# Halo copy on another engine, a fixed choice of Z buffers, and a last block taken tile by tile with two result buffers

## The chip, the cores and the metric

One core of one Trainium2 chip runs the whole program. Times are device microseconds of one launch, from the profiler or from timed runs. Of TensorE, VectorE, ScalarE, GpSimd and SyncE (which issues most DMAs) each has its own queue of instructions; they meet only at semaphores.

## The reference, cut to what matters

Two decoder layers with post-layernorm, on x of 2 x 2048 x 512 (T = 4096 rows). Six residual blocks follow each other. The change touches the last three: the Mamba block (its projection and convolution, and its scan), and the last two blocks, attention over a context of 77 rows and an int8 matmul, which the kernel runs as one stage.

```python
# Mamba block: d_inner = 1024, d_state = 16
x_in, z = split(x @ in_proj_w.T)
x_in = silu(conv1d(x_in, width 4, 3 zeros ahead of each sequence) + conv_b)
dt, Bp, Cp = split(x_in @ x_proj_w.T);  dt = clip(softplus(dt * w + b), 1e-4, 10)
h = h * exp(dt * A) + dt * Bp * x_in          # for 16 states n, over time
y = sum_n h[n] * Cp[n]
y = (layernorm(y) * ln_g + ln_b + D * x_in) * silu(z);  out = y @ out_proj_w.T
# last two blocks
x5 = layernorm(x + softmax(q k.T / sqrt(32)) v @ Wo + bo)      # 16 heads, 77 keys
q = round(x5 / s), s = max|x5| over the row / 127
x6 = layernorm(x5 + (q @ round(rhs / rs)) * s * rs)
```

## The kernel before, in words

Everything is written out by hand: each stage opens a block with one function per engine, and the order of the calls in these functions is the order on that engine. `wait_ge(semaphore, count)` holds an engine's queue in order. P = 128, D = 512, KD = D / 128 = 4, TB = 512, NU = 4.

**Input stage** (`inner_stage`, 8 blocks of 512 time steps, 8 channel groups c of 128). In round n TensorE transposes x of block n (L1706), projects it group by group (`project`, L1714), and between groups 0 and 1 computes x_proj of block n-1 (`x_proj`, L1722) and, behind group 1, spreads its dt (L1727). ScalarE copies the transposes (`copy_xt`, L1762) and the projections into xi (`copy_xi`, L1770), applies silu for block n-1 (`silus`, L1807), logs for n-2 and Abs, Relu and Exp for n-1 (`exps`). VectorE convolves (`conv`, L1905 and L1910): xi has room for 3 columns ahead of the 512 of a block, the halo, which must hold the last 3 columns of the block before. So ahead of the convolutions of block n VectorE copies it for all 8 groups in one instruction (L2021); for block 4, the first of the second sequence, it writes zeros (L2019). xi is double-buffered. GpSimd does the middle of the softplus for n-1 (L1850 to L1863) and the product with u for n-2 (L1868).

**Scan stage** (`scan_stage`, 4 time pieces of 1024, 8 groups, 16 states n: 512 scans). GpSimd makes X = B * w (L2255), ScalarE A = exp(dt * A) (L2277), VectorE scans (L2431). The sum over n of h * C is made in three ways: for n in 0, 3, 6, 9, 12 by TensorE out of transposes (`turn`, `fold`), for 4, 7, 10 by GpSimd into Z (`outputs`, L2262), for the eight others by VectorE into Z (L2436). TensorE adds each Z to PSUM (`add`, L2379). Z has RZ = 4 buffers; `zed(k)` numbers the 11 products of a group of 16, and keeps counting from group to group, `same_z(k)` names the product that used the buffer last, and `mm` counts TensorE's adds. A second branch (`clips == 1`), not taken in this data, already chooses the buffer by `zed(n)`.

**Final stage** (`final_stage`, 8 blocks of 512 rows, each 4 tiles of 128). In round n: attention of block n, residual, layernorm and quantising of block m = n-1, int8 result of block f = n-2. TensorE: `scores`, `project` (L2888), `turn`, `queries`, `values`, `int8` (transposes L2933, matmuls L2938). VectorE: `rescale` (y6 = big * scales, L3072), `add_x5` (L3076), `residual` (L3091), statistics of r5 and y6 (L3081), `aggregate` (L3097), `inverse` (L3103), `round5` (x5 L3107, maximum L3114, scales L3116 and L3118, q5 L3122 and L3125), and the normal of y6 (L3107). ScalarE: exps, copies, one Sqrt per round (L3002), casts of q5 (L2996). SyncE stores y6 when all four tiles of it are normalised (L2838). y6 is single: `rescale(f)` waits for the store of block f-1. `project(m, a)` waits for rescale of tile a of block m-1, since both use the PSUM bank big[a]. Rounds 8 and 9 only drain the pipeline: round 8 has project, residual and `round5` of block 7 and the result of block 6, round 9 the result of block 7.

Of the kernel before, what the change touches and what calls it, by code (L numbers as in the profile page):

```python
# [1593 lines left out]
def inner_stage(nc, x3_d, ident, win_t, conv_w, conv_b, xp_t, dtw, dtb, a_log, sel_b, keepA, flag, u_d, dt_d, w_d, xd_d, xt_d):  # L1594
# [3 lines left out]
    with ExitStack() as ctx:  # L1598
# [156 lines left out]
        def _(act):  # L1755
# [133 lines left out]
        def _(dve):  # L1889
# [176 lines left out]
def scan_stage(nc, keepA, flag, ident, win_t, dt_d, w_d, xd_d, xt_d, y_d, z_d):  # L2066
# [12 lines left out]
    with ExitStack() as ctx:  # L2079
# [167 lines left out]
        def _(pool):  # L2247
# [95 lines left out]
        def _(pe):  # L2343
# [25 lines left out]
            def add(k):  # L2369
# [8 lines left out]
                for e in range(TC // TB):  # L2378
                    last = nc.tensor.matmul(yp[:, e * TB:(e + 1) * TB], idn[:], Z[:, zed(k) % RZ, e * TB:(e + 1) * TB], start=(n == FIRST), stop=(n == NS - 1))  # L2379
# [29 lines left out]
        def _(dve):  # L2409
# [5 lines left out]
            with dve.If(clips == 0):  # L2415
                for k in range(NU_):
# [15 lines left out]
                    if on_dve(n):  # L2432
                        dve.wait_ge(sn, 1 + k + 1)
                        dve.wait_ge(mm, 1 + NS + (added(same_z(k)) if zed(k) >= RZ else 0))
                        dve.wait_ge(cc[ci(n)], 1 + (i + 1) * 16)
                        nc.vector.tensor_tensor(Z[:, zed(k) % RZ], a, Cm[:, ci(n)], ALU.mult).then_inc(cd, 1)  # L2436
# [326 lines left out]
def final_stage(nc, x4_d, ident, wq, bq, wo_, bo, rhs_t, keep, out_d):  # L2763
# [5 lines left out]
    with ExitStack() as ctx:  # L2769
# [16 lines left out]
        q5, y6 = s.sb("q5", [P, NU, D]), s.sb("y6", [P, NU, D])  # L2786
# [15 lines left out]
        qtr, qte, im, ia, ib, ok, stored = [s.sem(n) for n in ("qtr", "qte", "im", "ia", "ib", "ok", "stored")]  # L2802
# [4 lines left out]
        CPB = NB // B  # L2807

# [8 lines left out]
        def _(sp):  # L2817
# [14 lines left out]
            for n in range(1, NB + 2):  # L2832
# [3 lines left out]
                if n >= 2:  # L2836
                    sp.wait_ge(ok, 1 + (n - 1) * NU)
                    sp.dma_start(orr[n - 2], y6[:]).then_inc(stored, 16)  # L2838
            sp.wait_ge(stored, 1 + NB * 16)

        @block.gpsimd
        def _(pool):
# [3 lines left out]
            for n in range(NB):  # L2846
                for a in range(NU):
# [3 lines left out]
                    nc.gpsimd.tensor_tensor(x[:, n % NX_, a], x[:, n % NX_, a], bor[:], ALU.add).then_inc(xbo, 1)  # L2851

        @block.tensor
        def _(pe):
# [85 lines left out]

            queries(0)
            pe.wait_ge(keys, 1 + HB4 * B)
            for n in range(NB + 1):
# [13 lines left out]
                if n:  # L2957
# [5 lines left out]
        def _(act):  # L2963
# [39 lines left out]

            queries(0)
            for n in range(NB + 2):
# [5 lines left out]
                if slots(n):  # L3011
# [11 lines left out]
                elif n <= NB:  # L3023
                    integers(n - 1)

        @block.vector
        def _(dve):
# [39 lines left out]
            def rescale(f):  # L3067
                dve.wait_ge(stored, 1 + f * 16)
                dve.wait_ge(wte, 3)
                for a in range(NU):  # L3070
                    dve.wait_ge(im, 1 + f * NU + a + 1)
                    nc.vector.scalar_tensor_tensor(out=y6[:, a], in0=big[:, a], scalar=ls[:, a:a + 1], in1=rg[:], op0=ALU.mult, op1=ALU.mult).then_inc(ia, 1)  # L3072

            def add_x5(f, a):
                dve.wait_ge(ia, 1 + f * NU + a + 1)
                nc.vector.tensor_tensor(y6[:, a], y6[:, a], x5[:, a], ALU.add).then_inc(ib, 1)  # L3076
# [7 lines left out]
            def stats_y6(f, a):  # L3084
                dve.wait_ge(ib, 1 + f * NU + a + 1)
                stats_of(1, a, y6)
# [40 lines left out]
            for n in range(NB + 2):  # L3127
# [30 lines left out]
                if old:  # L3158
                    for a in range(NU):
                        normal(y6[:, a], y6[:, a], 1, a).then_inc(ok, 1)  # L3160
                if n == 0:
                    weights()

# [80 lines left out]
```

## Time and profile before

| what | value |
|---|---|
| median of 3 runs | 4980.63 us (4979.41 to 4981.1) |
| the profiled execution's own time | 4978.69 us |
| its span, first to last instruction | 4976.9 us |
| busy share TensorE, VectorE, ScalarE, GpSimd | 85%, 71%, 45%, 53% |
| mean granted TensorE clock | 0.935 |

The page divides the span by engine and in 40 slices; a share is an average over stages with different limits. The input stage lies at about 2160 to 2580 us, the scan at 2585 to 4100, the final stage at 4420 to 4977. A timeline row gives start, duration, engine, line, operation, result and operands, how many instructions are merged in it, and in brackets how long the engine idled before and what released it.

### The profile page before, as it was taken

What the parts mean: (1) busy time and instruction counts of PE and PEld (TensorE: products, weight loads), DVE (VectorE), ACT (ScalarE), POOL (GpSimd) and SP (SyncE); (2) the same over time, 40 slices, a digit from 0 to 9 for tenths busy, and PEclk for the clock granted to TensorE, in tenths of its full rate; (3) what the DMA queues carried; (4) which work ended last, traced back from release to release, by engine and by line L of the source; (5) the groups of instructions that cost most, each with busy time, mean ns of one, the idle gap of its engine ahead of it and who ended that gap; (6) DMA issues with size and microseconds to landing.
All of it is one profiled execution on the core that took longest, in us unless ns stands there. A gap on an engine that the chain in (4) does not pass through costs nothing. (4 is left out here: it accounts for less than half of the span.)

```text
span 4976.9 us, 49426 instructions
## 1 busy us (share of the span) xinstructions
PE 4217.4 (85%) x16117; PEld 2401.9 (48%) x16117; DVE 3526.9 (71%) x3880; ACT 2218.5 (45%) x3950; POOL 2654.5 (53%) x1555
## 2 busy tenths in 40 slices
PE   8997987599999459979837988888888888978886
PEld 6776875344444124433314555555555543435553
DVE  5554337522277555559978999999999997955676
ACT  1211114322255631037755676666766664423442
POOL 4544965100033011118868999999999986622221
PEclk9998996599999779989969999999999999989998
DMA  3332233242278765425453242242242217630100
GB/s 106 105 95 63 79 100 118 76 155 87 101 280 299 290 265 203 152 96 196 162 191 118 70 133 100 70 142 91 71 157 75 70 41 268 228 115 18 34 26 34
DMA packets 364162, 632.15 MB, mean 127 GB/s; under 512 B 67478, under 2 KB 153271, under 8 KB 351746
## 3 DMA queue, kind: packets, MB, share of 16 engines
q1 hardware_dynamic: 326850, 585.97, 33.7%
q10 hardware_dynamic: 37056, 43.00, 2.4%
q8 instruction: 132, 2.16, 0.2%
q14 instruction: 124, 1.02, 0.1%
HBM read 400.73 MB, written 228.15 MB: 126 GB/s over the span
## 5 line engine op out<-in xcount | busy, mean ns | idle before, releaser
L2255 POOL TENSOR_TENSOR sc_X<-sc_Bm,sc_w 128x1024 f32<-128x1024 f32 x512 | 1192.3, 2364 | 101.4 <-DVE sc_A L2431 42.1
L2379 PE MATMUL sc_yp<-sc_Z,sc_idn 128*128 128x512 f32 x1408 | 674.5, 602 | 23.2 <-DVE sc_Z L2436 21.4
L1329 PE MATMUL ff_ps<-ffn_R 128*128 128x512 f32 x1536 | 660.6, 592 | 0.7 <-issue 0.7
L2277 ACT ACTIVATE sc_A<-sc_dt,keep_A 128x1024 f32<-128x1024 f32 x512 | 575.2, 1123 | 162.4 <-DVE sc_Z L2436 84.2
L1329 PEld LDWEIGHTS ff_ps<-ffn_R 128*128 128x128 f32 x1536 | 291.2, 190 | 364.5 <-issue 363.8
L2307 ACT ACTIVATE sc_hT<-sc_tp,sc_ct 128x128 f32<-128x128 f32 x1280 | 362.8, 366 | 173.2 <-PE sc_tp L2359 172.2
L2379 PEld LDWEIGHTS sc_yp<-sc_Z,sc_idn 128*128 128x128 f32 x1408 | 248.5, 191 | 272.9 <-issue 209.1
L2366 PEld LDWEIGHTS sc_yp<-sc_idn,sc_hT 128*128 128x128 f32 x2560 | 306.6, 192 | 113.3 <-ACT sc_hT L2307 80.9
L2366 PE MATMUL sc_yp<-sc_idn,sc_hT 128*128 128x128 f32 x2560 | 318.1, 278 | 15.7 <-ACT sc_hT L2307 15.7
L2436 DVE TENSOR_TENSOR sc_Z<-sc_A,sc_Cm 128x1024 f32<-128x1024 f32 x256 | 313.5, 1225 | 8.9
L2431 DVE TENSOR_TENSOR_SCAN sc_A<-sc_A,sc_X 128x1024 f32<-128x1024 f32 x128 | 292.1, 2282 | 31.7 <-ACT sc_A L2277 28.9
L73 POOL TENSOR_TENSOR gp_pbd<-gp_r,gp_msk 128x512 f32<-128x512 f32 x144 | 182.2, 1265 | 236.4 <-DVE gp_r L474 236.4
L2431 DVE TENSOR_TENSOR_SCAN sc_A<-sc_A,sc_hc,sc_X 128x1024 f32<-128x1024 f32 x128 | 299.6, 2341 | 2.3 <-ACT sc_A L2277 2.3
L2359 PE MATMUL sc_tp<-sc_idn,sc_H 128*128 128x128 f32 x1280 | 196.0, 276 | 119.4 <-DVE sc_A L2431 71.7
L2431 DVE TENSOR_TENSOR_SCAN sc_H<-sc_A,sc_hc,sc_X 128x1024 f32<-128x1024 f32 x128 | 295.2, 2337 | 1.1 <-ACT sc_A L2277 1.1
L2431 DVE TENSOR_TENSOR_SCAN sc_H<-sc_A,sc_X 128x1024 f32<-128x1024 f32 x128 | 287.2, 2274 | 11.6 <-POOL sc_X L2255 11.6
L2388 PE MATMUL sc_zp<-sc_xz,sc_wz 128*128 128x512 f32 x512 | 266.0, 601 | 28.9 <-issue 17.8
L1357 PE MATMUL ff_ps<-ffn_downT,ffn_R 128*128 128x512 f32 x672 | 289.3, 593 | 0.4 <-DVE ffn_R L1538 0.4
L2359 PEld LDWEIGHTS sc_tp<-sc_idn,sc_H 128*128 128x128 f32 x1280 | 150.1, 141 | 286.6 <-issue 175.9
L1373 ACT ACTIVATE ff_o<-ff_ps,ff_scx 128x512 f32<-128x512 f32 x192 | 129.0, 683 | 333.5 <-PE ff_ps L1329 320.7
L2849 POOL TENSOR_TENSOR fi_pr<-fi_pr,fi_rp 128x1232 f32<-128x1232 f32 x32 | 71.9, 2248 | 375.2 <-DVE fi_rp L3065 375.2
L1453 DVE TENSOR_REDUCE ff_amg<-ff_o 128x1 f32<-128x512 f32 x96 | 65.5, 686 | 269.8 <-ACT ff_o L1373 269.7
(379 smaller groups left out, 8083.0 us busy)
## 6 DMA issues: line engine op xcount, KB each, us to landing
sc_Bm<-d_xd SPq DMA_DIRECT2D x64, 512.0 KB, 7.5
ffn_gate_d<-ff_o SPq DMA_DIRECT2D x96, 256.0 KB, 2.2
ffn_up_d<-ff_o SPq DMA_DIRECT2D x96, 256.0 KB, 6.3
ffn_g_d<-ff_z SPq DMA_DIRECT2D x24, 1024.0 KB, 6.7
ffn_R<-ffn_g_d SPq DMA_DIRECT2D x8, 3072.0 KB, 11.0
ffn_R<-ffn_up_d SPq DMA_DIRECT2D x8, 3072.0 KB, 21.6
ffn_R<-ffn_up_d SPq DMA_DIRECT2D x23, 1024.0 KB, 12.8
sc_Cm<-d_xd SPq DMA_DIRECT2D x44, 512.0 KB, 8.2
```

Of the source, the lines that this page charges most:

```text
L73: return eng.tensor_tensor(out.rearrange("p g (c m) -> p g c m", m=16), packed.unsqueeze(2).broadcast_to([P, n, CH, 16]), mask.rearrange(" ...
L1329: last = nc.tensor.matmul(ps[:, 2 + t % 6], w[:, k, h * P:(h + 1) * P], xt[:, n, k], start=(k == 0), stop=(k == KD - 1))
L1357: last = nc.tensor.matmul(ps[:, v * NU + u], zd[v][:, k, u * P:(u + 1) * P], downT[:, k], start=(k == 0), stop=(k == HB_ - 1))
L2255: nc.gpsimd.tensor_tensor(X[:, k % RX], Bm[:, n], w[:, j % 2], ALU.mult).then_inc(db, 1)
L2277: nc.scalar.activation(A[:, k % 2], dt[:, j % 2], ACT.Exp, scale=keepA[:, n:n + 1]).then_inc(ex, 1)
L2307: nc.scalar.activation(hT[:, q], tp[:, b * P:(b + 1) * P], ACT.Copy, scale=ct[:, i % 2, q, n:n + 1]).then_inc(tc, 1)
L2359: last = nc.tensor.transpose(tp[:, b * P:(b + 1) * P], H[:, slot(k % NS), h * TB + b * P:h * TB + (b + 1) * P], idn[:])
L2366: last = nc.tensor.matmul(yp[:, b * P:(b + 1) * P], hT[:, b], idn[:], start=False, stop=False)
L2379: last = nc.tensor.matmul(yp[:, e * TB:(e + 1) * TB], idn[:], Z[:, zed(k) % RZ, e * TB:(e + 1) * TB], start=(n == FIRST), stop=(n == NS - 1))
L2388: nc.tensor.matmul(zp[:], wz[:, q], xz[:, q], start=(q == 0), stop=(q == KD - 1)).then_inc(zm, 1)
L2431: nc.vector.tensor_tensor_scan(h, a, X[:, k % RX], 0.0 if first else hc[:, k % CU:k % CU + 1], ALU.mult, ALU.add).then_inc(sn, 1)
L2436: nc.vector.tensor_tensor(Z[:, zed(k) % RZ], a, Cm[:, ci(n)], ALU.mult).then_inc(cd, 1)
```

## The change

**Input stage.** ScalarE gets `copy_halo(n + 1)`, issued behind `copy_xi(n, 7)`, for all blocks but 0 and 4. VectorE keeps only the memset of block 4.

**Scan stage.** The Z buffer is `zed(n) % RZ`, so every group of 16 begins at buffer 0, in both branches, and `same_z(k)` is rewritten to match: buffers 0, 1, 2 have three users in a group, buffer 3 has two.

**Final stage.** y6 becomes two buffers, and `stored` two semaphores. The rounds 8 and 9 are replaced by an order written out per tile (`last_blocks` on VectorE, `last_int8` on TensorE, the list of roots and casts on ScalarE); each tile has its own aggregation, root, reciprocal, scales and quantising. The four adds of x5 for block 6 move to GpSimd. Block 7 is stored tile by tile.

```diff
+            def copy_halo(n):                              # input stage, ScalarE
+                act.wait_ge(rev, 1 + n * RG)
+                act.wait_ge(cv, 1 + (n - 1) * CB)
+                nc.scalar.copy(xi[:, n % 2, :, 0:3], xi[:, (n - 1) % 2, :, TB:TB + 3]).then_inc(halo, 1)
...
                         copy_xi(n, c)
+                    if c == CB - 1 and n + 1 < NB and n + 1 != NB // B:
+                        copy_halo(n + 1)
...
-                if n:
+                if n == NB // B:
                     dve.wait_ge(cv, 1 + (n - 1) * CB)
-                if n == NB // B:
                     nc.vector.memset(xi[:, n % 2, :, 0:3], 0.0).then_inc(halo, 1)
-                elif n:
-                    nc.vector.tensor_copy(xi[:, n % 2, :, 0:3], xi[:, (n - 1) % 2, :, TB:TB + 3]).then_inc(halo, 1)
...
         def same_z(k):
-            zs = [m for m in range(NS) if not on_pe(m)]
-            p = zs.index(k % NS) - RZ
-            return (k // NS + p // NZ) * NS + zs[p % NZ]
+            users = [m for m in range(NS) if not on_pe(m) and zed(m) % RZ == zed(k % NS) % RZ]
+            p = users.index(k % NS) - 1
+            return (k // NS + p // len(users)) * NS + users[p]
...
-                        nc.vector.tensor_tensor(Z[:, zed(k) % RZ], a, Cm[:, ci(n)], ALU.mult).then_inc(cd, 1)
+                        nc.vector.tensor_tensor(Z[:, zed(n) % RZ], a, Cm[:, ci(n)], ALU.mult).then_inc(cd, 1)
...
-        q5, y6 = s.sb("q5", [P, NU, D]), s.sb("y6", [P, NU, D])
+        q5, y6 = s.sb("q5", [P, NU, D]), s.sb("y6", [P, 2, NU, D])
...
+            for a in range(NU):                            # SyncE
+                sp.wait_ge(ok, 1 + F * NU + a + 1)
+                sp.dma_start(orr[F, :, a], y6[:, F % 2, a]).then_inc(stored[F % 2], 16)
...
+            for a in range(NU):                            # GpSimd, F = NB - 1
+                pool.wait_ge(ia, 1 + (F - 1) * NU + a + 1)
+                nc.gpsimd.tensor_tensor(y6[:, (F - 1) % 2, a], y6[:, (F - 1) % 2, a], x5[:, a], ALU.add).then_inc(ib, 1)
...
+                pe.wait_ge(res, 1 + NB * NU - 1)           # TensorE, last_int8
+                turn_q(0)
+                turn_q(1)
+                multiply(0)
+                multiply(1)
+                turn_q(2)
+                multiply(2)
+                pe.wait_ge(res, 1 + NB * NU)
+                turn_q(3)
+                multiply(3)
...
+            root_r5(0)                                     # ScalarE
+            root_r5(1)
+            root_y6(F - 1)
+            root_r5(2)
+            last_integer(0)
+            last_integer(1)
+            last_integer(2)
+            root_r5(3)
+            last_integer(3)
+            for a in range(NU):
+                root_y6(F, a)
...
+            def spread_r5(a):                              # VectorE; spread_y6 is its like
+                dve.wait_ge(res, 1 + F * NU + a + 1)
+                stats_of(0, a, r5)
+                dve.wait_ge(stats, 1 + counted[0])
+                nc.vector.bn_aggr(mv[:, 0, a], st[:, 0, a]).then_inc(eag, 1)
...
+            def last_blocks():
+                f = F - 1
+                rescale(f)
+                residual(F, 0)
+                spread_r5(0)
+                spread_y6(f, 0)
+                spread_y6(f, 1)
+                round_tile(0)
+                residual(F, 1)
+                spread_r5(1)
+                spread_y6(f, 2)
+                spread_y6(f, 3)
+                round_tile(1)
+                residual(F, 2)
+                spread_r5(2)
...
+                for a in range(NU):
+                    normal(y6[:, f % 2, a], y6[:, f % 2, a], 1, a).then_inc(ok, 1)
+                round_tile(2)
+                residual(F, 3)
+                spread_r5(3)
+                rescale_tile(F, 0)
+                add_x5(F, 0)
+                round_tile(3)
+                spread_y6(F, 0)
+                for a in range(1, NU):
+                    rescale_tile(F, a)
+                    add_x5(F, a)
+                    finish_tile(F, a - 1)
+                    spread_y6(F, a)
+                finish_tile(F, NU - 1)
```

`round_tile(a)` holds, for one tile, the reciprocal of the root, x5, its maximum, the two scales and the two quantising steps; `finish_tile(f, a)` the reciprocal and the normal of y6; each of their instructions waits for the one before.

## Rows read from the trace of the kernel before

**Rows 1.** Busy time by stretch, input stage: stretch, its length, busy us per engine.
```profile
core 0: us, PE busy (x) PEld busy (x) DVE busy (x) ACT busy (x) POOL busy (x), PEclk, DMA share, GB/s
2235.00:2282.00 47.00, 43.09 (x98) 17.39 (x98) 46.11 (x51) 34.07 (x56) 38.89 (x41) 0.90 0.50 180
...
2330.00:2373.00 43.00, 39.81 (x99) 15.98 (x97) 40.41 (x56) 33.94 (x57) 38.76 (x40) 0.96 0.55 197
```

**Rows 2.** The halo copy, by its line and as a group (count, busy, mean ns, idle).
```profile
L2021 DVE COPY in_xi<-in_xi x6: 173/7956/9009, 2192.5 to 2474.1; 128x24 f32<-128x24 f32 x6
...
L2021 DVE COPY in_xi<-in_xi 128x24 f32<-128x24 f32 x6 | 41.2, 6868 | 0.0
```

**Rows 3.** Timeline of VectorE in the input stage.
```profile
2287.51 7.24 DVE L2021 COPY in_xi<-in_xi 128x24 f32<-128x24 f32 x1
...
2334.80 0.08 DVE L2019 MEMSET in_xi<- 128x24 f32 x1
...
2376.51 8.87 DVE L2021 COPY in_xi<-in_xi 128x24 f32<-128x24 f32 x1
...
2520.66 0.75 DVE L1910 SCALAR_TENSOR_TENSOR in_acc<-in_xi,in_cw,in_ac 128x512 f32<-128x512 f32 x1
```

**Rows 4.** Timeline of GpSimd near the copy that begins at 2287.51.
```profile
2293.44 1.27 POOL L1858 TENSOR_TENSOR in_E<-in_E,in_Wm 128x512 f32<-128x512 f32 x1
2294.79 1.27 POOL L1863 TENSOR_TENSOR in_V<-in_V,in_E 128x512 f32<-128x512 f32 x1
```

**Rows 5.** Timeline of TensorE: first project matmuls of blocks 2, 4, 5, 7; transposes.
```profile
2235.04 6.67 PE L1714 MATMUL in_ps<-in_xt,in_win 128*128 128x512 f32 x8 [0.68 <-ACT in_xt L1762]
...
2329.58 5.40 PE L1714 MATMUL in_ps<-in_xt,in_win 128*128 128x512 f32 x8 [0.68 <-ACT in_xt L1762]
...
2371.11 1.14 PE L1706 MATMUL in_ps<-in_idn,in_x 128*128 128x128 f32 x8 [1.69 <-ACT in_xt L1762]
2372.93 3.70 PE L1714 MATMUL in_ps<-in_xt,in_win 128*128 128x512 f32 x8 [0.68 <-ACT in_xt L1762]
...
2468.87 3.70 PE L1714 MATMUL in_ps<-in_xt,in_win 128*128 128x512 f32 x8 [0.67 <-ACT in_xt L1762]
```

**Rows 6.** ScalarE's copies of one column, as a group.
```profile
L2289 ACT COPY sc_hc<-sc_H 128x1 f32<-128x1 f32 x49 | 9.6, 197 | 22.7 <-DVE sc_H L2431 20.2 <-ACT sc_yo L2313 2.4
```

**Rows 7.** Scan stage: the products into Z, and their timeline between two groups.
```profile
L2436 DVE TENSOR_TENSOR sc_Z<-sc_A,sc_Cm 128x1024 f32<-128x1024 f32 x256 | 313.5, 1225 | 8.9
...
3118.58 1.23 DVE L2436 TENSOR_TENSOR sc_Z<-sc_A,sc_Cm 128x1024 f32<-128x1024 f32 x1
...
3119.88 1.88 PE L2379 MATMUL sc_yp<-sc_Z,sc_idn 128*128 128x512 f32 x4
...
3131.40 1.23 DVE L2436 TENSOR_TENSOR sc_Z<-sc_A,sc_Cm 128x1024 f32<-128x1024 f32 x1
```

**Rows 8.** Timeline of the last rounds of the final stage.
```profile
4920.79 3.62 PE L2938 MATMUL fi_big<-fi_rq,fi_qbt 128*128 128x512 bf16 x16
...
4926.09 2.73 DVE L3072 SCALAR_TENSOR_TENSOR fi_y<-fi_big,fi_ls,fi_rg 128x512 f32<-128x512 f32 x4 [4.38 <-DMA out<-fi_y]
...
4926.98 15.67 PE L2888 MATMUL fi_big<-fi_wo,fi_att 128*128 128x512 f32 x32 [2.58 <-DVE fi_y L3072]
...
4932.39 0.69 DVE L3091 TENSOR_TENSOR fi_r<-fi_big,fi_x 128x512 f32<-128x512 f32 x1 [2.38 <-PE fi_big L2888]
...
4969.26 0.18 DVE L3103 RECIPROCAL fi_rstd<-fi_sd 128x4 f32<-128x4 f32 x1 [0.36 <-ACT fi_sd L3002]
4969.47 1.92 DVE L3107 TENSOR_SCALAR fi_y<-fi_y,fi_mv,fi_rstd 128x512 f32<-128x512 f32 x4
```

**Rows 9.** Groups of VectorE's instructions in the final stage.
```profile
L3081 DVE BATCH_NORM_STATS2 fi_st<-fi_y 128x6 f32<-128x512 f32 x32 | 20.3, 680 | 0.0
...
L3107 DVE TENSOR_SCALAR fi_y<-fi_y,fi_mv,fi_rstd 128x512 f32<-128x512 f32 x32 | 15.3, 545 | 0.0
```

**Rows 10.** DMA issues: count, KB each, median us to landing.
```profile
d_dt<-in_Wm SPq DMA_DIRECT2D x25, 256.0 KB, 2.3
...
out<-fi_y SPq DMA_DIRECT2D x2, 1024.0 KB, 4.3
```

More of the change, by code:

```diff
@@ L2378, in add @@
                 for e in range(TC // TB):
-                    last = nc.tensor.matmul(yp[:, e * TB:(e + 1) * TB], idn[:], Z[:, zed(k) % RZ, e * TB:(e + 1) * TB], start=(n == FIRST), stop=(n == NS - 1))
+                    last = nc.tensor.matmul(yp[:, e * TB:(e + 1) * TB], idn[:], Z[:, zed(n) % RZ, e * TB:(e + 1) * TB], start=(n == FIRST), stop=(n == NS - 1))
                 last.then_inc(mm, 1)
@@ L2801, in final_stage @@
             "om", "res", "stats", "aggr", "root", "rsd", "x5ok", "la", "lb", "lc", "qa", "qk")]
-        qtr, qte, im, ia, ib, ok, stored = [s.sem(n) for n in ("qtr", "qte", "im", "ia", "ib", "ok", "stored")]
+        qtr, qte, im, ia, ib, ok = [s.sem(n) for n in ("qtr", "qte", "im", "ia", "ib", "ok")]
+        stored = [s.sem(f"stored{v}") for v in range(2)]
+        eag, ert, ers, ex5, ela, elb, elc, eqa, eqk, eyg, eyt, eys = [s.sem(n) for n in (
+            "eag", "ert", "ers", "ex5", "ela", "elb", "elc", "eqa", "eqk", "eyg", "eyt", "eys")]
         s.start()
@@ L2807, in final_stage @@
         CPB = NB // B
+        F = NB - 1
         def slots(n):
@@ L2939, in int8, with last_int8, turn_q, multiply @@
                     last.then_inc(im, 1)
+            def last_int8():
+                def turn_q(a):
+                    pe.wait_ge(eqk, 1 + a + 1)
+                    for k in range(KD):
+                        last = nc.tensor.transpose(big[:, a, k * P:(k + 1) * P], q5[:, a, k * P:(k + 1) * P], idn[:])
+                    last.then_inc(qtr, 1)
+                def multiply(a):
+                    pe.wait_ge(qte, 1 + F * NU + a + 1)
+                    for k in range(KD):
+                        last = nc.tensor.matmul(big[:, a], qbt[:, a, k], rq[:, k], start=(k == 0), stop=(k == KD - 1))
+                    last.then_inc(im, 1)
+                pe.wait_ge(res, 1 + NB * NU - 1)
[8 more added lines that the diff above has]
+                multiply(3)
             queries(0)
@@ L2956, in _ @@
                     values(n)
-                if n:
+                if n == NB:
+                    last_int8()
+                elif n:
                     int8(n - 1)
@@ L3002, in roots, with root_r5, root_y6, last_integer @@
                 nc.scalar.activation(sd[:, used], mv[:, used, :, 1], ACT.Sqrt, bias=eps[:]).then_inc(root, 1)
+            def root_r5(a):
+                act.wait_ge(eag, 1 + a + 1)
+                nc.scalar.activation(sd[:, 0, a:a + 1], mv[:, 0, a, 1:2], ACT.Sqrt, bias=eps[:]).then_inc(ert, 1)
+            def root_y6(f, a=None):
+                us = slice(0, NU) if a is None else slice(a, a + 1)
+                act.wait_ge(eyg, 1 + NU + (0 if a is None else a + 1))
+                nc.scalar.activation(sd[:, 1, us], mv[:, 1, us, 1], ACT.Sqrt, bias=eps[:]).then_inc(eyt, 1)
+            def last_integer(a):
+                act.wait_ge(im, 1 + F * NU)
+                act.wait_ge(qtr, 1 + F * NU + a + 1)
+                nc.scalar.copy(qbt[:, a].rearrange("p k t -> p (k t)"), big[:, a]).then_inc(qte, 1)
             queries(0)
-            for n in range(NB + 2):
+            for n in range(NB + 1):
                 if n < NB:
@@ L3010, in _ @@
                     turned(n, 1)
-                if slots(n):
+                if slots(n) and n < NB:
                     roots(n)
@@ L3125, in round5, with spread_y6 @@
                     nc.vector.tensor_scalar(q5[:, a], q5[:, a], MAGIC, None, ALU.subtract).then_inc(qk, 1)
-            for n in range(NB + 2):
+            def spread_r5(a):
[3 more added lines that the diff above has]
+                nc.vector.bn_aggr(mv[:, 0, a], st[:, 0, a]).then_inc(eag, 1)
+            def spread_y6(f, a):
+                stats_y6(f, a)
+                dve.wait_ge(stats, 1 + counted[0])
+                nc.vector.bn_aggr(mv[:, 1, a], st[:, 1, a]).then_inc(eyg, 1)
@@ new lines, in round_tile @@
+            def round_tile(a):
+                dve.wait_ge(ert, 1 + a + 1)
+                nc.vector.reciprocal(rstd[:, 0, a:a + 1], sd[:, 0, a:a + 1]).then_inc(ers, 1)
+                dve.wait_ge(ers, 1 + a + 1)
+                dve.wait_ge(ib, 1 + (F - 1) * NU + a + 1)
+                normal(x5[:, a], r5[:, a], 0, a).then_inc(ex5, 1)
+                dve.wait_ge(ex5, 1 + a + 1)
+                nc.vector.tensor_reduce(lm[:, a:a + 1], x5[:, a], AX.X, ALU.max, apply_absolute_value=True).then_inc(ela, 1)
+                dve.wait_ge(ela, 1 + a + 1)
+                nc.vector.tensor_scalar(ls[:, a:a + 1], lm[:, a:a + 1], 1e-12, 1.0 / 127.0, ALU.max, ALU.mult).then_inc(elb, 1)
+                dve.wait_ge(elb, 1 + a + 1)
+                nc.vector.reciprocal(li[:, a:a + 1], ls[:, a:a + 1]).then_inc(elc, 1)
+                dve.wait_ge(elc, 1 + a + 1)
+                dve.wait_ge(qtr, 1 + F * NU)
+                nc.vector.tensor_scalar(q5[:, a], x5[:, a], li[:, a:a + 1], MAGIC, ALU.mult, ALU.add).then_inc(eqa, 1)
+                dve.wait_ge(eqa, 1 + a + 1)
+                nc.vector.tensor_scalar(q5[:, a], q5[:, a], MAGIC, None, ALU.subtract).then_inc(eqk, 1)
@@ new lines, in finish_tile @@
+            def finish_tile(f, a):
+                dve.wait_ge(eyt, 1 + 1 + a + 1)
+                nc.vector.reciprocal(rstd[:, 1, a:a + 1], sd[:, 1, a:a + 1]).then_inc(eys, 1)
+                dve.wait_ge(eys, 1 + 1 + a + 1)
+                normal(y6[:, f % 2, a], y6[:, f % 2, a], 1, a).then_inc(ok, 1)
[14 more added lines that the diff above has]
+                spread_r5(2)
+                dve.wait_ge(eyt, 2)
+                nc.vector.reciprocal(rstd[:, 1], sd[:, 1]).then_inc(eys, 1)
+                dve.wait_ge(eys, 2)
+                for a in range(NU):
+                    normal(y6[:, f % 2, a], y6[:, f % 2, a], 1, a).then_inc(ok, 1)
+                round_tile(2)
[11 more added lines that the diff above has]
+                finish_tile(F, NU - 1)
@@ L3128, in _ @@
+            for n in range(NB):
                 m, f = n - 1, n - 2
```

30 lines of the change are left out of this document (17 added, 13 removed).

## The prediction

> **What bounds the kernel now.** The diff touches three stages, so I read first the busy time of each engine in stretches of those stages, and then, inside a stretch, the timeline of the engine with the least idle time. In the Mamba input stage (about 2160 to 2580 us) VectorE is busy for 46.1 of 47 us in a block that begins with a halo copy, and for 40.4 of 43 us in block 4, which has a memset in its place [rows 1]. VectorE is the bound there. The copy moves 24 numbers per partition; it takes 173 ns once and up to 9009 ns otherwise, 41.2 us for all six [rows 2]. What the reader is to see in the two timelines: the copy begun at 2287.51 lasts 7.24 us, to 2294.75, and GpSimd, back to back until then, has a gap just from 2294.71 to 2294.79 [rows 3, 4]. The copy waits for GpSimd to pause; the 173 ns one is the first, at 2192.5, when GpSimd had no work yet.
>
> In the scan stage the 256 products of VectorE into Z have 8.9 us of idle time before them, 0.035 us each, and no releaser is named: that is the price of depending on the instruction before, not a wait for a buffer [rows 7]. In the final stage the y6 buffer costs something only at the end: rescale of block 6 idles 4.38 us for a store [rows 8], that of block 7 about as long again, and then four tiles go through each step together, so that TensorE, ScalarE and VectorE take turns.
>
> **Part 1, halo copy to ScalarE.** Six copies leave VectorE; five of them were stalled, 41.2 - 0.2 = 41.0 us together [rows 2]. All of it is saved only while VectorE stays the bound, so what is late next? TensorE's rounds (first project matmul of a block to that of the next) tell: from block 4 to 5, where nothing stalls VectorE, 2372.93 - 2329.58 = 43.35 us; the five rounds from block 2 to 7 take 2468.87 - 2235.04 = 233.8 us, so the other four 47.6 on average [rows 5]. Within a round TensorE and ScalarE hand over to each other: transposes wait 1.69 us for ScalarE's xt copies [rows 5], and x_proj for all eight silus. VectorE, when in time, has no part in it, so 43.35 us is the next bound.
>
> The new copy stands between ScalarE's last xi copy and its last exps, ahead of those xt copies, so its whole length is added to a round. What it waits for is there already: ScalarE's own xi copies, and the convolutions of the block before, for which its silus have waited earlier in the round. Queued behind it are one exps group and the xt copies. ScalarE's copy of a single column takes 197 ns [rows 6]; for 24 columns and the wait for its own last write I take 0.3 us (nearest to that row; bounds 0.2 and, three times the row, 0.6). The round of block 4 began with eight matmuls in 5.40 us, that of block 5 with 3.70 [rows 5], a clock matter that x_proj's wait for the silus mostly absorbs; so I use 43.5 us. Five rounds are 217.5 us, gain 16.3. In block 7 the last convolution ended at 2520.66 + 0.75 = 2521.4, 52.5 us after its round began; in block 4 that span is 2376.51 - 2329.58 = 46.9 us [rows 3, 5]; gain 5.6. Together 21.9; with block 2 begun 0.3 us later and something lost behind, 21. All that follows (silu, x_proj, softplus, stores) hangs on that last convolution, so the gain reaches the end of the stage. Bounds: rounds of 45.05 us (43.35 + 1.7, the clock's part not absorbed) give 8.5 + 5.6 = 14; with VectorE still the bound and block 4's idle time of 41.7 - 40.4 = 1.3 us back in each of five blocks, 41.0 - 6.5 = 34.
>
> Here a rule speaks against me. The traced copy outlasts single GpSimd instructions, of 1.27 us each [rows 3, 4]. The Trainium skill (SBUF — State Buffer, section SBUF: two separate sides) says that VectorE and GpSimd share a port pair under an exclusive lock, kept for one whole instruction, while ScalarE never waits for another engine. The second half would make the plan work. By the first half the port explains one GpSimd instruction per copy at most, 5 x 1.27 = 6 us of the 41, and the rest would be the copy's own and could move along with it; an estimate by it is a gain of 6 us here in place of 21. I follow the trace.
>
> **Part 2, Z buffers chosen by n.** Eleven products per 16 states rotate over four buffers. Now every group starts again at buffer 0, so its first three writes (n = 1, 2, 4) wait for an add three writes back, not four. For n = 1 that is the add of n = 13. Product 13 runs from 3118.58, its add from 3119.88 to 3121.76, and the next group's first product begins at 3131.40 [rows 7]: 9.6 us to spare. n = 2 waits for 14, both about 4 us later, and n = 4 is GpSimd's and later still. Cost 0, hidden by the scans of VectorE in between; each microsecond of TensorE's lag beyond 9.6 would count 31 times. A gain is excluded, as nothing waited.
>
> **Part 3, final stage.** (a) Two y6 buffers: rescale of block 6 starts when TensorE's first product is there, about 4921.7, not at 4926.09, and block 7's project follows the int8 products at once, at 4920.79 + 3.62 = 4924.4 in place of 4926.98 [rows 8]. Its first tile took 5.41 us (to 4932.39) with slow matmuls after 2.58 us of idling; without that idling eight take 3.7 [rows 5, 8]. So the first residual starts at 4928.1 (4929.8 if the clock drops all the same). The four adds of x5 for block 6 go to GpSimd, done by about 4928 while VectorE waits for TensorE: hidden, at some 1.3 us each.
> (b) From there VectorE is the bound, with TensorE and ScalarE beside it tile by tile. Its work, each instruction behind the one before, 0.035 us added: 4 residuals, 12 statistics, 4 maxima, 4 adds and 4 rescales, all near the statistics' 0.68 us [rows 9], 28 x 0.71 = 19.9; 12 aggregations, 9 reciprocals and 8 scale operations near the 0.18 us reciprocal [rows 8], together 5.5; 8 single normals at 0.57 [rows 9] and 4 in 1.92 us [rows 8], 6.5; 8 quantising steps at that 0.48, 3.8; one wait for ScalarE's root, 0.4 [rows 8]. Sum 36.1, end 4964.2. The last product is in time: tile 3's integers leave VectorE near 4953, transposes, cast and matmuls of one tile take under 4 us, and its rescale comes near 4960.
> (c) Now the last normals end at 4969.47 + 1.92 = 4971.4 [rows 8] and the span 5.5 us later, behind a store of 1024 KB that lands in 4.3 us; one of 256 KB lands in 2.3 [rows 10]. New end 4964.2 + 5.5 - 2.0 = 4967.7, gain 9.2. Bounds: 4 (clock down, 1.7, and 0.05 us more for each of some 70 waits, 3.5) and 11 (the small operations as short as in groups now).
>
> **Sum.** The profiled execution took 4978.69 us around a span of 4976.9. 4978.7 - 21 - 9.2 = 4948.5. It stands 1.9 us under the median of 4980.63, so I expect a median of 4950.5.
>
> **The rivals.** 1: VectorE stays the bound, rounds near 41.7 us. For it: its own pace in block 4 [rows 3]. Against: TensorE's 43.35 at the same place. Gain 34 + 9: 4937.5.
> 2: the rounds stretch, by TensorE's clock, a ScalarE copy of 0.6 us (4 x 0.3 more) or GpSimd's chain (38.8 of 43 us busy in block 4 [rows 1]). Rounds near 45.3, gain 13 here and 7 at the end: 4960.5. Against: block 4 shows all three engines at the fast pace once.
> 3: the copy is slow by itself. 7 to 9 us then stand inside TensorE's round in four of the five, 51 us each: 4 x 51 + 43.4 = 247 against 233.8, 5.6 back, 9 at the end: 4979, no change. For it: it outlasts single GpSimd instructions. Against: the 173 ns [rows 2].
> 4, the other side: Z's shorter distance. Place: the first product of each group. Price: 31 times what TensorE lags beyond 9.6 us. From 1.0 us per group it eats the gain, from 1.3 the kernel is slower by 10 us; with 1.5 us it is 4950 + 47 = 4997. For it: TensorE is close to full in the scan. Against: the add begins 0.07 us after its product ends [rows 7].
>
> **Chances.** Forecast 0.64, rival 1 0.13, rival 2 0.17, rival 3 0.03, rival 4 0.03. The range is 4938 to 4963, from about rival 1 to just past rival 2 and to the poor bounds of both gains (14 + 4). A change under 0.2% (10 us) can't be told from none here. Faster 0.94, the same 0.04 (rival 3 and a sliver of 2), slower 0.02.
>
> **What would show it.** No copy on VectorE in the input stage, six on ScalarE of 0.2 to 0.3 us; TensorE's rounds at 43 to 44 us, VectorE idling some 2 us per block for xi; the last convolution 21 us earlier; Z products as before; project of block 7 right behind the int8 products at the full clock; the last normal 7 us earlier counted from the stage's start. I am wrong if ScalarE's copies take microseconds, if rounds stay at 47 us, or if TensorE gates Z.

## The result, and the profile after

The changed kernel takes 4949.78 us (median of 4 runs, 4948.61 to 4953.84) against 4980.86 us (4 runs, 4979.41 to 4982.02) of the kernel before: a ratio of 0.9941, 95% interval 0.9929 to 0.9953. That is 31 us less. The profiled execution took 4948.61 us around a span of 4946.8, which is 30.1 less than before. Medians, where given, are of all runs and ratios of the undisturbed ones; three runs in the whole study were disturbed, at 5914.69 and 13430.14 us with the tensor_scalar copy below and at 5926.08 us of the kernel before beside it.

I set the same events of both traces beside each other. Each line is a stretch between two events, in us, of one profiled execution of each kernel.

| stretch, from event to event | before | after | change |
|---|---|---|---|
| start of the trace to the first convolution's last step | 2167.81 | 2165.55 | -2.3 |
| to the start of the last convolution's last step | 352.85 | 333.15 | -19.7 |
| to the first scan | 75.62 | 75.40 | -0.2 |
| to the last scan | 1496.40 | 1495.70 | -0.7 |
| to the first matmul of the final stage | 336.74 | 337.55 | +0.8 |
| to the final stage's last table load on ScalarE | 478.37 | 481.75 | +3.4 |
| to the end of the last normal | 63.60 | 54.34 | -9.3 |
| to the end of the span | 5.51 | 3.36 | -2.2 |

The input stage. Busy time of two rounds of TensorE, as in [rows 1]; the columns are stretch, length, busy time of TensorE, its weight loads, VectorE, ScalarE and GpSimd, TensorE's granted clock, the DMA share and GB/s:

```profile
2233.12:2277.26 44.14, 41.29 (x99) 16.72 (x99) 38.97 (x53) 34.60 (x58) 39.11 (x40) 0.93 0.53 192
...
2321.00:2364.00 43.00, 39.96 (x98) 16.30 (x98) 39.25 (x54) 34.20 (x58) 39.21 (x41) 0.96 0.54 197
```

VectorE is down from 46.1 us to 39.0 in a block with a halo copy. The copy itself, now on ScalarE, by its line and as a group, the answer to [rows 2]:

```profile
L1776 ACT COPY in_xi<-in_xi x6: 218/218/221, 2187.1 to 2447.4; 128x24 f32<-128x24 f32 x6
...
L1776 ACT COPY in_xi<-in_xi 128x24 f32<-128x24 f32 x6 | 1.3, 219 | 0.2
```

TensorE's transposes and first project matmuls of its rounds, the answer to [rows 5]:

```profile
2233.12 6.58 PE L1714 MATMUL in_ps<-in_xt,in_win 128*128 128x512 f32 x8 [0.68 <-ACT in_xt L1762]
2275.43 1.15 PE L1706 MATMUL in_ps<-in_idn,in_x 128*128 128x128 f32 x8 [1.93 <-ACT in_xt L1762]
2277.26 6.70 PE L1714 MATMUL in_ps<-in_xt,in_win 128*128 128x512 f32 x8 [0.68 <-ACT in_xt L1762]
2319.45 1.15 PE L1706 MATMUL in_ps<-in_idn,in_x 128*128 128x128 f32 x8 [1.69 <-ACT in_xt L1762]
2321.26 5.19 PE L1714 MATMUL in_ps<-in_xt,in_win 128*128 128x512 f32 x8 [0.68 <-ACT in_xt L1762]
2364.47 3.70 PE L1714 MATMUL in_ps<-in_xt,in_win 128*128 128x512 f32 x8 [0.68 <-ACT in_xt L1762]
2405.85 1.67 PE L1706 MATMUL in_ps<-in_idn,in_x 128*128 128x128 f32 x8 [1.93 <-ACT in_xt L1762]
2408.19 6.09 PE L1714 MATMUL in_ps<-in_xt,in_win 128*128 128x512 f32 x8 [0.68 <-ACT in_xt L1762]
2452.25 6.25 PE L1714 MATMUL in_ps<-in_xt,in_win 128*128 128x512 f32 x8 [0.68 <-ACT in_xt L1762]
```

The five rounds are 44.14, 44.00, 43.21, 43.72 and 44.06 us, 43.83 on average. The halo copy shows directly: where there is one, the transposes wait 1.93 us for ScalarE's xt copies, where there is none (ahead of block 4) 1.69. What lies over 43.2 goes with slow matmuls about the start of a round: three rounds begin with eight matmuls in 6.1 to 6.7 us in place of 3.7 (granted clock of the first round shown 0.93, of the one of 43.21 us 0.96), and the round of 43.72 us, which begins with 3.70, ends with eight transposes in 1.67 us in place of 1.15.

VectorE now waits for ScalarE's xi at the head of every block, where it had 0.9 us of idle time in a whole block [rows 1]; the rows are its first convolution step of blocks 3 and 4:

```profile
2284.62 0.81 DVE L1913 TENSOR_SCALAR in_ac<-in_xi,in_cw,in_cb 128x512 f32<-128x512 f32 x1 [3.95 <-ACT in_xi L1770]
...
2327.30 0.81 DVE L1913 TENSOR_SCALAR in_ac<-in_xi,in_cw,in_cb 128x512 f32<-128x512 f32 x1 [2.36 <-ACT in_xi L1770]
```

The scan stage. The 256 products into Z, against [rows 7]:

```profile
L2441 DVE TENSOR_TENSOR sc_Z<-sc_A,sc_Cm 128x1024 f32<-128x1024 f32 x256 | 313.5, 1225 | 8.8
```

The end of the final stage, against [rows 8]: the timeline from rescale of block 6 to the last normal, and the four stores.

```profile
4903.61 2.96 DVE L3143 SCALAR_TENSOR_TENSOR fi_y<-fi_big,fi_ls,fi_rg 128x512 f32<-128x512 f32 x4 [0.61 <-PE fi_big L2955]
4904.44 4.94 POOL L2868 TENSOR_TENSOR fi_y<-fi_y,fi_x 128x512 f32<-128x512 f32 x4 [10.30 <-DVE fi_y L3143]
4905.54 13.90 PE L2905 MATMUL fi_big<-fi_wo,fi_att 128*128 128x512 f32 x32
4909.18 0.69 DVE L3162 TENSOR_TENSOR fi_r<-fi_big,fi_x 128x512 f32<-128x512 f32 x1 [2.61 <-PE fi_big L2905]
4909.90 0.69 DVE L3152 BATCH_NORM_STATS2 fi_st<-fi_r 128x6 f32<-128x512 f32 x1
4910.63 0.18 DVE L3202 BATCH_NORM_AGGREGATE fi_mv<-fi_st 128x2 f32<-128x6 f32 x1
4910.73 0.66 DVE L3152 BATCH_NORM_STATS2 fi_st<-fi_y 128x6 f32<-128x512 f32 x1
...
4942.69 0.16 DVE L3229 RECIPROCAL fi_rstd<-fi_sd 128x1 f32<-128x1 f32 x1 [0.36 <-ACT fi_sd L3054]
4942.89 0.55 DVE L3178 TENSOR_SCALAR fi_y<-fi_y,fi_mv,fi_rstd 128x512 f32<-128x512 f32 x1
```

```profile
out<-fi_y SPq DMA_DIRECT2D x4, 256.0 KB, 2.0
```

Rescale no longer waits for a store, project follows the int8 products at the full clock (13.90 us for 32 matmuls at a granted clock of 1.00, before 15.67 at 0.89), and from 4909.18 on VectorE has a single idle time that a releaser ends, the 0.36 us ahead of the last reciprocal.

One stretch got longer although the change hardly touches it: from the first matmul of the final stage to the last table load. Its first 22 us differ in the granted clock, 0.95 before and 0.80 after (the third number from the end; the first row is of the kernel before, the second of the changed one):

```profile
4430.00:4452.00 22.00, 19.12 (x55) 10.00 (x53) 1.34 (x1) 6.38 (x9) 0.00 (x0) 0.95 0.60 222
```

```profile
4408.00:4430.00 22.00, 20.50 (x51) 10.39 (x50) 0.00 (x0) 6.22 (x9) 0.00 (x0) 0.80 0.59 219
```

Over all profiles of this study that stretch takes 478.1 to 478.9 us ten times and 481.4 to 481.9 four times. The first 22 us after the stage's first matmul have a granted clock of 0.79 in those four and of 0.92 to 0.94 in the ten. All four are of kernels with the new final stage, but five more kernels with it are among the ten. And nearly all of the difference is there by the stage's first residual, which starts 90.4 to 90.6 us after the first matmul in the four and 86.9 to 87.9 in the ten. Up to there no instruction that reads or writes y6 has run. So I don't count the 3.4 us as a price of the new code; why the clock falls early in some executions and not in others stays open.

### The profile page after: what moved, and what is told of

It reads as the page before. It is cut to its first block and busy times, and to the rows that moved or that the text cites. A ratio compares the mean times of both kernels' runs of the same rounds, so it can differ in the third digit from the quotient of the medians.

```text
span 4946.8 us, 49497 instructions
## 1 busy us (share of the span) xinstructions
PE 4213.3 (85%) x16109; PEld 2399.2 (48%) x16117; DVE 3486.8 (70%) x3883; ACT 2222.8 (45%) x3963; POOL 2659.8 (54%) x1559
## 3 DMA queue, kind: packets, MB, share of 16 engines
q8 instruction: 132, 2.16, 0.2%
```

## Experiments: the parts by themselves

Times are medians beside runs of the kernel before on the same chip. Totals of one kernel scatter by some 5 us to either side, so I also give the input stage (the second line of the table, 352.85 us before) and the tail (the seventh, 63.60 us).

**Halo copy alone**: `inner_stage` of the changed kernel, all else as before.

> The kernel before with the halo copy on ScalarE alone. My theory: this is two thirds of the gain. Its input stage is that of the changed kernel (TensorE's rounds near 43.8 us, last convolution about 20 us earlier counted from the stage's start), time 4961. Rival (the final stage or the Z buffers bring the main part, the input stage's gain is lost in the scan): under 8 us, time 4973 or more.

4963.31 us, ratio 0.9967 (0.9954 to 0.9979), 16.8 us less; input stage 334.07 us, tail 63.54. The part gives its 18.8 us of the input stage where it was expected.

**Final stage alone**: `final_stage` of the changed kernel.

> The kernel before with the new final stage alone. My theory: the tail from the last root table load of the steady rounds to the end is 57.7 us in place of 69.1, so 11.4 us less, time 4969.5. Rival (part of that is luck of the clock at the start of the last blocks): 7 to 9 us less, 4972 to 4974.

4970.03 us, ratio 0.9982 (0.9972 to 0.9992); input stage 351.67, tail 54.36 us, and 3.4 us from the last normal to the end of the span in place of 5.5. As expected.

**Z buffers alone**: `scan_stage` of the changed kernel.

> The kernel before with the Z buffers chosen by n alone. My theory: nothing waits, the scans from first to last take 1496.4 us as before, time 4980.9 within 2. Rival (the shorter distance costs, but is hidden in the sum by another gain): each microsecond of wait per group is 31 us, so 4985 or more, with idle time ahead of the products into Z above 8.9 us.

4980.06 us, ratio 1.0001 (0.9991 to 1.001). Its 256 products have 8.9 us of idle time, as in [rows 7]. No cost, no gain. The tail of this profile is 65.32 us with the old final stage, where three others with that stage have 63.5 to 63.6: from 4902 to 4928 us TensorE's granted clock was 0.67, in the kernel before 0.99. So the old tail moves by 1.7 us with the clock; all nine new ones lie within 54.28 to 54.37 us.

**Two y6 buffers alone**, in the old order of the rounds:

```diff
-        q5, y6 = s.sb("q5", [P, NU, D]), s.sb("y6", [P, NU, D])
+        q5, y6 = s.sb("q5", [P, NU, D]), s.sb("y6", [P, 2, NU, D])
...
-                dve.wait_ge(stored, 1 + f * 16)
+                dve.wait_ge(stored[f % 2], 1 + f // 2 * 16)
```

> The kernel before with two y6 buffers and nothing else: order, whole-block store and engines as they were. My theory: block 7's project starts 2.6 us earlier and at the full clock (1.9 us more), and the last rescale starts when its first product is there: old 4960.96 against products from 4957.3, so 2 to 3 us; together 5 to 7 us of the 11.4, time 4974 to 4976. Rival (the per-tile order brings nearly all, the buffers only uncover other waits): 0 to 2 us, 4979 to 4981.

4972.2 us, ratio 0.9991 (0.9982 to 1.0001). The median is 8.0 us lower, more than the 5 to 7 expected, but the interval of the ratio just takes in 1, so the runs alone don't tell this from no change. The trace tells more. The tail is 58.04 us, 5.6 less than before, within the 5 to 7 expected, and VectorE idles 0.25 us ahead of rescale, for TensorE's product, not 4.38 us for a store:

```profile
4920.76 3.24 DVE L3074 SCALAR_TENSOR_TENSOR fi_y<-fi_big,fi_ls,fi_rg 128x512 f32<-128x512 f32 x4 [0.25 <-PE fi_big L2940]
```

So of the 9.3 us of the tail the second buffer gives 5.6 and the rest of the new final stage, the order tile by tile with the four adds on GpSimd, 3.7; these last two were not run apart. Behind the tail the small stores give 2.1: with one store for the block this run still takes 5.6 us from the last normal to the end.

## Experiments: why the copy was slow, and what bounds the rounds now

The reduction, the lighter GpSimd, the added VectorE work and the copy between the xt copies were timed on another chip, where the kernel before took 4978.4 us; across chips the ratios compare, not the times.

**Another instruction for the copy, on VectorE.** A reduction over an axis of one element moves the same 24 numbers, at the old place in VectorE's queue:

```diff
-                    nc.vector.tensor_copy(xi[:, n % 2, :, 0:3], xi[:, (n - 1) % 2, :, TB:TB + 3]).then_inc(halo, 1)
+                    nc.vector.tensor_reduce(xi[:, n % 2, :, 0:3], xi[:, (n - 1) % 2, :, TB:TB + 3].unsqueeze(3), AX.X, ALU.max).then_inc(halo, 1)
```

(the rest is the changed kernel without `copy_halo` on ScalarE)

> The changed kernel with the halo back on VectorE, but as a tensor_reduce over an axis of one element, which computes the same. Theory A (the old copy waited because GpSimd and a two-port copy exclude each other; VectorE now has 2 to 4 us to spare per block): the six reductions take about 0.2 us each, rounds are 0.24 us shorter than in the changed kernel (ScalarE freed), time 4949 to 4950, about 1 us less. Rival (any VectorE operation from SBUF to SBUF at that place, or this access pattern, stalls): 5 to 9 us each, rounds of 47 us, time 4970.

4946.37 us, ratio 0.9935 (0.9921 to 0.9948), input stage 330.90 us.

```profile
L2020 DVE TENSOR_REDUCE in_xi<-in_xi x6: 173/174/176, 2194.2 to 2457.1; 128x24 f32<-128x24 f32 x6
```

All six take 173 to 176 ns beside the same GpSimd work. So neither the data, nor the access pattern, nor the place, nor a wait for the convolutions is enough to make such an instruction slow, and moving it to ScalarE was not needed for the gain. The interval overlaps the changed kernel's; its rounds are shorter in the trace (below).

**The copy kept, GpSimd lightened.** The kernel before, with `less_one`, `lost` and `relu_plus` on 8 of 512 columns, so most of the softplus is left out.

> The kernel before, where GpSimd's less_one, lost and relu_plus in the input stage work on 8 of 512 columns (the softplus is left incomplete), so that GpSimd has gaps while the halo copy is due; the copy stays a VectorE copy. Theory (the copy waits for GpSimd's first gap): copies of 0.2 to 1.3 us, rounds of 43 to 44 us, and more saved at the end of the stage where GpSimd shares the work: time 4960 or less. Rival (the copy is slow by itself in a full pipeline, for its access pattern or for DMA traffic): still 7 to 9 us each, rounds of 47 us, gain at the stage's end only, 4970 to 4978.

4948.47 us, ratio 0.9937 (0.9922 to 0.9952); input stage 330.91 us (the stretch behind it shortens too, from 75.6 to 67.7 us, with the lighter softplus, so 8 us of the total aren't the copy's).

```profile
L2021 DVE COPY in_xi<-in_xi x6: 173/174/175, 2194.9 to 2457.7; 128x24 f32<-128x24 f32 x6
```

The very instruction that took up to 9009 ns takes 174. The stall comes from GpSimd's work. This run answers a second question: its five rounds take 217.0 us together, as with the reduction beside the full GpSimd work (217.0). So GpSimd is not what bounds the rounds now.

**Is it the copy, or a class?** The same place, once as `tensor_scalar(..., 1.0, None, ALU.mult)`, once as `tensor_tensor(x, x, ALU.max)`.

> The changed kernel with the halo copy on VectorE once more, written as tensor_scalar (times 1.0) of the same 24 numbers, one input from SBUF. Known by now: as a copy it takes 7 to 9 us while GpSimd works, as a tensor_reduce 0.17 us at the same place. Theory: the stall belongs to the plain elementwise forms of VectorE with one fp32 input (copy and tensor_scalar alike), not to the name of the instruction; then five of the six take 7 to 9 us again, the rounds of TensorE average 46 to 47 us, and the time is about 4968 to 4971 (only the final stage's gain is left). Rival: it is the copy alone; then 0.17 us each, rounds of 43.0 to 43.9 us, 4946 to 4950.

> The same place, the halo copy as tensor_tensor (maximum of the 24 numbers with themselves), two inputs from SBUF. Theory: such an instruction waits for one GpSimd instruction at most, as the 1.0 to 1.2 us that small tensor_tensors of 128x8 take near 2555 us suggest where their like takes 0.16; then 0.2 to 1.3 us each, VectorE's idle time of 2.4 to 4 us per block covers it, and the time is 4946 to 4951. Rival: it waits for a gap of GpSimd like the copy; 7 to 9 us each, about 4968 to 4971.

4970.36 us (ratio 0.998, 0.997 to 0.999) and 4969.56 us (0.998, 0.9971 to 0.9989); input stages 351.50 and 352.89 us.

```profile
L2020 DVE TENSOR_SCALAR in_xi<-in_xi x6: 174/7270/9021, 2190.7 to 2470.9; 128x24 f32<-128x24 f32 x6
```

```profile
L2020 DVE TENSOR_TENSOR in_xi<-in_xi x6: 177/8000/9004, 2195.5 to 2477.0; 128x24 f32<-128x24 f32 x6
```

The first came as expected; for the second my theory fell: two inputs wait as long as one. What all have in common is where they end. Here VectorE's instruction and GpSimd's around it:

```profile
2236.65 9.02 DVE L2020 TENSOR_SCALAR in_xi<-in_xi 128x24 f32<-128x24 f32 x1
```

```profile
2243.15 1.26 POOL L1863 TENSOR_TENSOR in_V<-in_V,in_E 128x512 f32<-128x512 f32 x1
2244.37 1.27 POOL L1858 TENSOR_TENSOR in_E<-in_E,in_Wm 128x512 f32<-128x512 f32 x1
2245.71 1.27 POOL L1863 TENSOR_TENSOR in_V<-in_V,in_E 128x512 f32<-128x512 f32 x1
```

GpSimd's instructions start before the one ahead of them has ended (2243.15 + 1.26 is past 2244.37), until the last two of a block, where L1863 depends on L1858 and there are 0.07 us between them (2245.64 to 2245.71). VectorE's instruction ends at 2245.67, inside that gap. It is so for all 30 stalled ones, five each of the kernel before, of these two, and of the kernels with the final stage, the Z buffers and the two y6 buffers alone: they end at this one pair of lines, whenever they began. Most lie across 8 or 10 GpSimd instructions and last 7.2 to 9.1 us; one, begun later, lies across 6 and lasts 6.0. VectorE's 512-column instructions in the same stage are not held at all. In the kernel before the middle convolution steps take 0.756 us in the median both where GpSimd is busy throughout (80 of them) and where it is idle (23), and the tensor_scalar of L1933 takes 0.685 against 0.682. Why these pass and the 24-number ones wait stays open; none of these runs varied the shape.

**More work on VectorE.** The changed kernel, with three reductions of 128 x 512 on a scratch tile behind `extremes(m)`.

> The changed kernel with three more reductions of 0.68 us (2.0 us) on VectorE in each of seven blocks of the input stage, on a scratch tile, with no one waiting for them. Theory (TensorE and ScalarE set the rounds, VectorE idles 2.4 to 4 us ahead of each block): rounds unchanged, VectorE's idle time before a block 2 us shorter; only block 7 and what follows it see their 2 us; time 2 us above the changed kernel. Rival (VectorE is the bound still): 7 x 2.0 = 14 us more.

4949.79 us, ratio 0.9938 (0.9923 to 0.9953); the five rounds take 219.9 us together, 219.1 in the changed kernel. The input stage takes 335.95 us, 2.8 more, of which about 2 were expected in block 7, with no next round to hide in; 14 in all would have come had VectorE been the bound. VectorE's idle time took up the rest:

```profile
2374.75 0.82 DVE L1917 TENSOR_SCALAR in_ac<-in_xi,in_cw,in_cb 128x512 f32<-128x512 f32 x1 [2.13 <-ACT in_xi L1772]
```

Still 2.1 us idle here and 1.2 to 2.1 at the other heads, with about 2.0 us of work added per block (0.67 us each): VectorE is not the bound.

**Less work on ScalarE**, on top of the reduction: Abs and Exp of channel group 7 on 8 of 512 columns from the third block on, which leaves out part of the softplus.

> Halo as a reduction on VectorE, and ScalarE's Abs and Exp of channel group 7 on 8 of 512 columns from the third block on: this leaves out part of the softplus of that group. These two stand between the last xi copy of a round and the silus, and shrink by about 0.5 us each. Theory: the hand-over between ScalarE and TensorE bounds the rounds, so those at the full clock shorten from 42.95 to about 41.9 us for the blocks concerned, four or five of them: some 4 to 5 us less in the input stage, time about 4942 to 4944. Rival: VectorE (its work is 41.7 us in a block without halo copy) or GpSimd bounds as well; then the rounds stay within 0.3 us of 42.95 and the time at 4946 to 4948.

4941.93 us, ratio 0.9927 (0.9912 to 0.9943); input stage 325.49 us. Three starts of rounds (block 4 to 6), and two of the kernel with the full Abs and Exp (blocks 5 and 6):

```profile
2322.24 3.70 PE L1714 MATMUL in_ps<-in_xt,in_win 128*128 128x512 f32 x8 [0.68 <-ACT in_xt L1762]
2364.35 3.70 PE L1714 MATMUL in_ps<-in_xt,in_win 128*128 128x512 f32 x8 [0.67 <-ACT in_xt L1762]
2406.47 3.70 PE L1714 MATMUL in_ps<-in_xt,in_win 128*128 128x512 f32 x8 [0.68 <-ACT in_xt L1762]
```

```profile
2367.59 5.15 PE L1714 MATMUL in_ps<-in_xt,in_win 128*128 128x512 f32 x8 [0.68 <-ACT in_xt L1762]
2410.54 3.70 PE L1714 MATMUL in_ps<-in_xt,in_win 128*128 128x512 f32 x8 [0.68 <-ACT in_xt L1762]
```

42.11 us against 42.95, so 0.84 less. From start to start the shortened Abs and Exp take 0.26 and 0.10 us in place of 0.67 and 0.52, together 0.83 less: what is taken from ScalarE between the last xi copy and the silus comes off the round. ScalarE with its hand-over to TensorE is the bound.

**The copy between the xt copies**: `copy_halo(n)` on ScalarE behind the second xt copy, where ScalarE would wait for TensorE's transposes anyway.

> The changed kernel with ScalarE's halo copy moved from behind the last xi copy to between the second and third xt copy of the next block, where ScalarE idled 0.26 us. Theory (rounds are set by the hand-over of TensorE and ScalarE, and the copy is on it where it stands now): TensorE's wait for xt falls from 1.93 to 1.69 us, rounds shorten by up to 0.24 us, 1 us in all, time 4949; the copy's 0.2 us may show ahead of the last xt copies, then nothing. Rival (VectorE is the bound): no change, and VectorE's waits for xi as they are.

4951.37 us, ratio 0.9945 (0.9931 to 0.9958); input stage 329.93 us, the shortest with all the work in it. Its rounds are 43.91, 42.96, 43.21, 43.72 and 42.96: 42.96 without the lower clock, against 43.21 in the changed kernel. The 0.25 us of the copy are gone from the round; 4951.37 us is not below the 4949 expected, and a total that scatters by 5 us can't show so little.

**Tail: more for GpSimd.** On top of the reduction, the four normals of block 6 and one addition of block 7 move from VectorE to GpSimd:

```diff
+            pool.wait_ge(eys, 2)
+            for a in range(NU):
+                nc.gpsimd.tensor_scalar(y6[:, (F - 1) % 2, a], y6[:, (F - 1) % 2, a], mv[:, 1, a, 0:1], rstd[:, 1, a:a + 1], ALU.subtract, ALU.mult).then_inc(okg, 1)
+            pool.wait_ge(ia, 1 + F * NU + 1)
+            nc.gpsimd.tensor_tensor(y6[:, F % 2, 0], y6[:, F % 2, 0], x5[:, 0], ALU.add).then_inc(ib, 1)
```

> Halo as a reduction on VectorE (4946.4 measured), and in the tail of the final stage five more operations on GpSimd, which is idle there: the four normals of y6 of block 6 (1.92 us of VectorE) and the addition of x5 to tile 0 of block 7 (0.6 us). Theory: VectorE is the bound of the tail, so the stretch from ScalarE's last table load to the last normal shrinks from 54.4 by 2.4 to 2.5 us, to 51.9, and the time to about 4944. Rival: while GpSimd works for some 2.5 us on the normals, VectorE's single normals and quantising steps stall behind it, up to those 2.5 us; then 54 to 54.5 us and no change against 4946.4.

4947.95 us, ratio 0.9937 (0.9924 to 0.9951); tail 54.28 us in place of 54.37. Nothing gained, where 2.4 to 2.5 us were expected. The rival's time came, but only in part by its cause:

```profile
L2869 POOL TENSOR_SCALAR fi_y<-fi_y,fi_mv,fi_rstd 128x512 f32<-128x512 f32 x4 | 8.6, 2156 | 13.7 <-DVE fi_rstd L3252 13.7
```

```profile
4924.21 0.95 DVE L3226 TENSOR_SCALAR fi_q<-fi_x,fi_li 128x512 f32<-128x512 f32 x1
...
4932.12 0.69 DVE L3155 BATCH_NORM_STATS2 fi_st<-fi_y 128x6 f32<-128x512 f32 x1 [1.22 <-POOL fi_y L2871]
```

A normal takes GpSimd 2.16 us, VectorE 0.48. The addition of tile 0 queues behind the four and VectorE waits 1.22 us for it. Before that a reciprocal waits 0.30 us for its root, and VectorE's own steps stretch beside GpSimd, the quantising one to 0.95 from 0.49.

## Why the prediction was right, point by point

The forecast was 4950.5 us within 4938 to 4963; measured 4949.8. Its steps:

**The copy waits for GpSimd to pause** [rows 3, 4]: shown, from both sides. Without GpSimd's long instructions it takes 174 ns, and 30 stalled ones end at the same gap. Why a reduction of the same numbers does not wait was not in the prediction.

**On ScalarE 0.3 us**: 0.22 us each. The transposes' wait grew from 1.69 to 1.93, so the whole length stands in the round, as said. The extrapolation from a one-column copy of 197 ns [rows 6] was good.

**Rounds of 43.5 us, then TensorE and ScalarE as the bound**: 43.83 on average, 5 x 0.33 = 1.6 us too short a forecast. The copy cost less than I allowed, but I had said that x_proj's wait absorbs most of a slow start of TensorE. That holds for a start of 5.19 us, whose round took 43.21; rounds that begin with eight matmuls in 6.1 to 6.7 us take 44.00 to 44.14, and slow transposes at a round's end (1.67 us in place of 1.15) made the one of 43.72. The gain of the stage was 19.7 us where I had 21. That ScalarE is half of this bound is shown by the shortened exps; VectorE's slack was 2.4 to 4.1 us per block, where I had said some 2. Block 7: 2498.70 + 0.75 - 2452.25 = 47.2 us against my 46.9.

**The rule that spoke against it.** Both the gain by the trace's reading (21) and the other one (6) were on the table; 19.7 was measured. The trace differs from the Trainium skill (SBUF — State Buffer, section SBUF: two separate sides), which has the lock of the shared ports kept for one whole instruction: here one VectorE instruction sits out 6 to 10 of GpSimd's. Its other half, that ScalarE does not wait, agrees with 218 to 221 ns for all six.

**Z at no cost**: 8.8 us of idle time in the 256 products, before 8.9, and 4980.06 against 4980.15 us alone.

**The first residual at 4928.1**: counted from the last table load (18.69 us earlier) it came at 4909.18 + 18.69 = 4927.9. Project ran at the full clock.

**VectorE's chain of 36.1 us**: it was 4943.44 - 4909.18 = 34.3. This is the term that was mis-sized, by 1.8 us. The 28 instructions near 0.71 us came to 19.9, as charged. The 29 small ones took 4.5 us where I had 5.5: eleven of the twelve aggregations cost 0.10 us, since the next instruction, which doesn't need them, starts before they end (4910.63, 4910.73). The twelve normals took 6.1 for 6.5 and the eight quantising steps 3.5 for 3.8, in part for the same reason: the second quantising step of a tile costs 0.34 us and a single normal of y6 0.46. My 5.5 also was not what I had said: 29 times 0.18 + 0.035 is 6.2. My own bound for this, a gain of 11 with the small operations as short as in groups, was the better value.

**The store, 2.0 us less**: 2.15.

**The sum** is thus 21 + 9.2 = 30.2 forecast and 30.1 measured in the spans, but two errors stand against each other: the tail gave 11.4 and the input stage 19.7, and the clock's 3.4 us at the start of the final stage were partly made up by 2.3 us ahead of the input stage, neither of them a gain or a price of the change. That the sum came out within 0.1 us is luck; each term by itself was within 2.2 us. The three parts run alone give 16.8 + 10.1 + 0.1 = 27.0 by their medians, within their intervals of the whole 31.

**The rivals.** VectorE as the bound: no, it idles at each block's head. Stretched rounds of 45.3: no, but a part of it came: TensorE's clock made four of the five rounds 0.5 to 0.9 us longer than 43.21. GpSimd's chain had no part in it, as the lighter GpSimd shows. The copy slow by itself: no. The distance in Z: no.

## What to carry to other kernels

A short VectorE instruction that takes microseconds beside a busy GpSimd is waiting for it: look at whether its end falls into GpSimd's next gap, and try another instruction for the same data before moving the work to another engine. When a stall goes, price the gain by the next engine's pace in a block that never had the stall; here that one block gave 43.35 us and the outcome was 43.8. And ask of each instruction in a written-out chain whether the next one depends on it, since that decides between 0.10 and 0.2 us.

## What the runs showed of the hardware that I had not expected

- The reduction of 24 numbers takes 173 to 176 ns where the copy, tensor_scalar and tensor_tensor of the same numbers take 6.0 to 9.1 us.
- These last not for one GpSimd instruction but for 6 to 10 in a row, up to a gap of 0.07 us, while VectorE's 512-column convolution steps take the same 0.756 us beside a busy and an idle GpSimd.
- GpSimd's tensor_scalar on 128 x 512 takes 2.16 us with two operands per partition; with constants (the softplus's `one_plus` of the changed kernel) it takes 0.64 on average.
- The final stage up to its last table load came out as either 478.1 to 478.9 or 481.4 to 481.9 us, with nothing between.
